# The first attention's start: order of loads, a key mask built on the chip, and the place of batch 1's work

## The reference, cut to what matters

```python
x = x + _L0_xattn_ref(_layernorm(x), ctx_4096, ctx_4096, Wq, Wk, Wv, Wo)
# inside: 32 query heads of 16, 8 key/value heads of 16, each shared by 4 query heads
q = (query @ Wq).reshape(b, sq, 32, 16).transpose(0, 2, 1, 3)
k = (key @ Wk).reshape(b, sk, 8, 16).transpose(0, 2, 1, 3)
v = (value @ Wv).reshape(b, sk, 8, 16).transpose(0, 2, 1, 3)
k, v = jnp.repeat(k, 4, axis=1), jnp.repeat(v, 4, axis=1)
probs = jax.nn.softmax(jnp.einsum('bhqd,bhkd->bhqk', q, k) * 16 ** -0.5, axis=-1)
out = jnp.einsum('bhqk,bhkd->bhqd', probs, v)      # then merged and multiplied by Wo
```

## Time and profile before

| | |
|---|---|
| median of 3 runs | 1506.38 us (1503.81, 1506.38, 1508.53) |
| the profiled execution's own time | 1510.69 us |
| its span in the trace | 1508.9 us, 31382 instructions |
| busy, whole span | PE 92%, VectorE 72%, ScalarE 51%, GpSimd 48% |
| first attention | starts the program; its last work ends near 170.8 us |

### The profile page before, as it was taken

The page is one execution under the profiler, slowest core; times in us unless marked ns, Lnnn a source line. Parts: engine busy times, 40 slices in busy tenths (PEclk is TensorE's granted clock), DMA queues, the critical chain, the costliest instruction groups (busy, mean ns, idle before and its releaser), DMA issues.

```text
span 1508.9 us, 31382 instructions
## 1 busy us (share of the span) xinstructions
PE 1392.4 (92%) x11352; PEld 831.1 (55%) x11352; DVE 1080.5 (72%) x2125; ACT 762.5 (51%) x2476; POOL 721.8 (48%) x748
## 2 busy tenths in 40 slices
PE   5898699997999999897999999999999788889998
PEld 5676344445777777544655555555555334434444
DVE  7998655645666666767989888898877888965212
ACT  4777363222434333347666666666665457655111
POOL 4887452001434443855666666666665405734000
PEclk9999699999999999999999999999999899999999
DMA  7999672124999988766766665756534401646000
GB/s 192 188 173 169 130 179 43 32 39 116 179 186 188 172 139 138 133 145 156 155 150 112 114 112 110 144 112 111 110 71 80 133 3 29 131 84 112 22 8 28
DMA packets 524569, 174.62 MB, mean 116 GB/s; under 512 B 482576, under 2 KB 507600, under 8 KB 524416
## 3 DMA queue, kind: packets, MB, share of 16 engines
q1 hardware_dynamic: 524416, 172.62, 59.3%
HBM read 53.27 MB, written 2.10 MB: 37 GB/s over the span
## 4 chain that ended last, share of the span: by engine, by line
PE 70%; DVE 10%; POOL 7%; issue 4%; DMA 4%; ACT 3%; SPq 1%; DVEq 0%; PEld 0%; ACTq 0%; POOLq 0%; PEldq 0%
PE bank L70 22%; PE bank L72 22%; PE bank L71 22%; DMA a_p_t<-a_p_hl 2%; PE bank L2787 1%; DVE stats L111 1%; POOL a_p_hl L691 1%; DVE a_negmax L595 1%; DVE a_p_hl L602 1%; POOL x_o_prod L3108 1%; POOL x_o_prod L3109 1%; POOL down_flat L3351 1%; POOL x_state L3101 1%; DMA a_q_t<-a_q_hl 0%; PE bank L1025 0%
## 5 line engine op out<-in xcount | busy, mean ns | idle before, releaser
L1913 POOL TENSOR_TENSOR a_q_ss<-a_q_ss,half 128x4 f32<-128x4 f32 x64 | 90.2, 1409 | 167.4 <-DVE a_q_ss L1822 83.9
L1735 ACT ACTIVATE a_probs<-a_masked,a_negmax 128x128 f32<-128x128 f32 x256 | 99.7, 391 | 101.4 <-DVE a_negmax L1793 101.4
L70 PE MATMUL bank<-a_wq_hi,xn_pair 128*128 128x512 f16 (+1 forms) x384 | 140.2, 365 | 7.9 <-DVE a_kn L1827 3.1
L1256 POOL TENSOR_TENSOR a_p_hl<-a_probs,a_p_hl 128x512 f16<-128x512 f32 x64 | 74.4, 1164 | 143.2 <-DVE a_p_hl L1180 143.2
L71 PE MATMUL bank<-a_wq_lo,xn_pair 128*128 128x512 f16 (+1 forms) x384 | 139.9, 364 | 0.0
L72 PE MATMUL bank<-a_wq_hi,xn_pair 128*128 128x512 f16 (+1 forms) x384 | 139.9, 364 | 0.0
L70 PE MATMUL bank<-a_wo_hi,a_o_hi 128*128 128x512 f16 x256 | 97.8, 382 | 4.4 <-DVE x_state L1809 3.5
L72 PE MATMUL bank<-a_wo_hi,a_o_lo 128*128 128x512 f16 x256 | 97.7, 382 | 0.0
L71 PE MATMUL bank<-a_wo_lo,a_o_hi 128*128 128x512 f16 x256 | 97.6, 381 | 0.0
L1928 POOL TENSOR_TENSOR a_normal<-a_probs,a_recip 128x512 f32<-128x512 f32 x64 | 90.3, 1410 | 5.0
L691 POOL TENSOR_TENSOR a_p_hl<-a_probs,a_p_hl 128x512 f16<-128x512 f32 x64 | 77.3, 1219 | 25.4 <-DVE a_p_hl L602 19.3
(11 more groups left out here) (467 smaller groups left out, 5029.9 us busy)
## 6 DMA issues: line engine op xcount, KB each, us to landing
a_no<-in_L_xattn_Wo SPq DMA_DIRECT2D x9, 1024.0 KB, 6.0
a_nq<-in_L_xattn_Wq SPq DMA_DIRECT2D x8, 1024.0 KB, 5.8
a_n_wq<-in_L_xattn_Wq SPq DMA_DIRECT2D x4, 768.0 KB, 5.1
a_n_wo<-in_L_xattn_Wo SPq DMA_DIRECT2D x4, 768.0 KB, 5.6
a_nk<-in_L_xattn_Wk SPq DMA_DIRECT2D x9, 256.0 KB, 3.0
a_nv<-in_L_xattn_Wv SPq DMA_DIRECT2D x9, 256.0 KB, 4.0
f_v_hat<-in_L_ffn_w SPq DMA_DIRECT2D x2, 1152.0 KB, 6.2
x_state<-in_x SPq DMA_DIRECT2D x8, 256.0 KB, 4.8
```

The costliest lines, as they stand in the source:

```text
L70: pe.matmul(out, lh, rh, start=start, stop=False)
L1256: pool.tensor_tensor(p_hl[s % PN][:, 1, t, :], probs[unit(s, t) % PROBS][:, :, :].rearrange("p h n -> p (h n)"), p_hl[s % PN][:, 0, t, :], ...
L1735: m = act.activation(probs[s % 2][:, h, :], src, ACT.Exp, bias=negmax[s % 2][:, h:h + 1], accum_out=total[s % 2][:, h:h + 1])
L1913: pool.tensor_tensor(r[:, :], r[:, :], K.half[:, 0:n], ALU.pow).then_inc(root_done.sem, 1)
```

## The change

The constants of batches 1 and 2 get delays (LATE), used through late_at in place of at for five kinds of step: batch 1's normalising moves from t = -8 to -3, its rows from -6 to -2, its context from -5 to -1, its keys on the PE from -1 to 2, their high half on ScalarE from -2 to 3, their masking from -1 to 3; batch 2's normalising from 0 to 3 and its rows from 2 to 4. The statistics of batches 2 and 3 move from t = -2 to 2. Batch 1's x and context are loaded at t = -13, behind the first transpose and the value weight; the transpose of batch 1 now stands behind the output weight's load. The last two quarters of the query weight are split at t = -11, ahead of batch 0's keys. The mask is no longer loaded: GpSimd makes a 128 x 8 tile with a memset and two affine selects, each waiting for the one before, ahead of its other constants, and the product reads each of its values 128 times. Steps of batches 3 to 7 keep their places.

```diff
-    WEIGHTS = (-13, -12, -11, -10, -9, -7, 2, 3, 4, 5)
+    WEIGHTS = (-13, -12, -11, -11, -11, -7, 2, 3, 4, 5)
+    LATE = {"norm": {1: 5, 2: 3}, "rows": {1: 4, 2: 2}, "ctx": {1: 4}, "keys": {1: 3}, "keys split": {1: 5}, "mask": {1: 4}}
-    R1, R2, R3 = -9, -2, 11
-    LX1, LV, LX2, LO, LX4 = -16, -14, -6, -6, 4
+    R1, R2, R3 = -9, 2, 11
+    LX1, LV, LX2, LO, LX4 = -13, -14, -6, -6, 4
-        keep = sb("keep", [P, KV, P], F16)
+        keep = sb("keep", [P, KV], F16)
+        late_at = lambda t, offset, kind: [b for b in range(B) if t == offset + UNITS * b + LATE[kind].get(b, 0)]
...
-            sp.dma_start(keep[:, :, :], keep_in).then_inc(keep_here, 16)
...
-                for b in at(t, KPROJ):
+                for b in late_at(t, KPROJ, "keys"):
                     keys(b)
...
                 if b == 0:
-                    dve.wait_ge(keep_here, 16)
+                    dve.wait_ge(keep_done, 3)
...
                     r = dve.tensor_tensor(k_m[b % 2][:, a, :, :], k_hl[b % 2][:, a, :].unsqueeze(1).to_broadcast([P, KV, P]),
-                                          keep[:, :, :], ALU.mult)
+                                          keep[:, :].unsqueeze(2).to_broadcast([P, KV, P]), ALU.mult)
...
             roots(0)
+            pool.memset(keep[:, :], 1.0).then_inc(keep_done, 1)
+            pool.wait_ge(keep_done, 1)
+            pool.affine_select(out=keep[:, :], in_=keep[:, :], compare_op=ALU.is_ge, fill=0.0,
+                               base=0, pattern=[[-D, KV]], channel_multiplier=1).then_inc(keep_done, 1)
+            pool.wait_ge(keep_done, 2)
+            pool.affine_select(out=keep[:, :], in_=keep[:, :], compare_op=ALU.is_ge, fill=0.0,
+                               base=D - 1, pattern=[[D, KV]], channel_multiplier=-1).then_inc(keep_done, 1)
```

More of the change, by code:

```diff
@@ L179, in load_first, with first_attention @@
         sp.dma_start(self.n2[:, :, :], self.w2.rearrange("(f p) d -> p f d", p=P)[:, 0:2, :]).then_inc(self.first_in, 16)
-def first_attention(K, front, x_in, ctx_t, keep_in, wq, wk, wv, wo):
+def first_attention(K, front, x_in, ctx_t, wq, wk, wv, wo):
     nc = K.nc
@@ L249, in first_attention @@
         max_done, plo_done, mixed = per_unit("max"), per_unit("plo"), per_unit("mixed")
-        const_done, ones_done, keep_here = sem("const"), sem("ones"), sem("keep_in")
+        const_done, ones_done, keep_done = sem("const"), sem("ones"), sem("keep")
         two = lambda n: [sem(f"{n}{i}") for i in range(2)]
@@ L339, in _ @@
                     load_context(1)
-                for b in at(t, XLO):
+                for b in late_at(t, XLO, "rows"):
                     turn_queries_in(b)
@@ L348, in _ @@
                         load_x(b)
-                for b in at(t, CTX):
+                for b in late_at(t, CTX, "ctx"):
                     if b + 2 < B:
@@ L498, in _ @@
                     high_of_queries(b)
-                for b in at(t, KSPLIT):
+                for b in late_at(t, KSPLIT, "keys split"):
                     high_of_keys(b)
@@ L634, in _ @@
                     low_of_values(b)
-                for b in at(t, KMASK):
+                for b in late_at(t, KMASK, "mask"):
                     masked_keys(b)
@@ L642, in _ @@
                         take_stats(b0, b1)
-                for b in at(t, CTX):
+                for b in late_at(t, CTX, "ctx"):
                     high_of_context(b)
-                for b in at(t, XHI):
+                for b in late_at(t, XHI, "rows"):
                     high_of_rows(b)
@@ L650, in _ @@
                     add_to_x(b)
-                for b in at(t, NORM):
+                for b in late_at(t, NORM, "norm"):
                     normalise(b)
@@ L3699, in stage_0_to_1 @@
         front = Front(K, c, *(a[f"L0_ffn_{w}"] for w in ("c1_w", "c2_w", "w1", "w2t")))
-        first_attention(K, front, a["x"], a["ctx_t"], a["keep"], *(a[f"L0_xattn_{w}"] for w in ("Wq", "Wk", "Wv", "Wo")))
+        first_attention(K, front, a["x"], a["ctx_t"], *(a[f"L0_xattn_{w}"] for w in ("Wq", "Wk", "Wv", "Wo")))
         K.end_stage()
@@ L3750, in tables @@
     vspec[P - 1] = np.stack([np.cos(rest).sum(0), -np.sin(rest).sum(0)])
-    keep = np.broadcast_to((i[:, None] // 16 == np.arange(8))[:, :, None], (P, 8, P)).astype(np.float16)
     f = lambda v: np.ascontiguousarray(v, np.float32)
     return {"hadamard": np.stack([h, -h], axis=1), "spec": f(spec), "inv": f(inv), "pspec": f(pspec),
-            "oinv": f(oinv), "keep": keep, "vspec": f(vspec)}
+            "oinv": f(oinv), "vspec": f(vspec)}
 def laid_out(inputs):
```

## The result

The changed kernel takes 1515.5 us (median of 6 runs, 1513.3 to 1518.8) against 1507.9 for the kernel before on the same chip (6 runs): a ratio of 1.005, 95% interval 1.0038 to 1.0061, so 5.7 to 9.2 us slower. Forecast were +6.2 us, 1512.6 us by the sum, and a slower kernel.

What follows compares the result with a forecast made beforehand. VectorE's pace was taken to bound the first attention from some 27 us on. -0.4 (fill) + 7.6 (14 products) - 1.0 (waits) = +6.2 us on 1506.4, so 1512.6; own range +3.7 to +9.1, all cases 1506.0 to 1517.0.

Steps and rivals of the forecast that it cites:

- The price of the mask: VectorE's masking products: each goes from 679 to 1220 ns with the mask standing still; 14 of them cost 7.6 us.
- Rival A: The masking product keeps its 679 ns, so only the fill counts: 1506.0 us; chance 0.12.
- The waits that would give 1.0 us back: VectorE's 2.5 us of waits for batches' keys and values shrink by 1.0 us, bounds 0 and 2.5.
- rival C: GpSimd's next subtraction goes between the two products of a pair, 1.15 us each for three pairs: +10.7 us, 1517.1; chance 0.11.
- Rival B: Product takes 1220 ns, but VectorE's shrinking waits for GpSimd and others absorb much of it: +1.0 us, 1507.4; chance 0.15.
- The fill: Start of the first attention, rearranged: worth 0.4 us (-0.4), bounds 2.5 us won to 1.5 us lost.
- Rival D: The first maxima's 3.2 us gain lasts to the end, product at 679 ns: -4.2 us, 1502.2; chance 0.03.
- The first transpose: Ahead of the first query projection: 1.1 to 1.4 us won, 0.45 to 0.7 lost; projection starts about 12.2, 0.5 us sooner.

Runs made afterwards that it cites:

- e2: The kernel before with only the small mask, built by GpSimd and read standing still, start order unchanged; ratio 1.0067 to before.
- e1: The changed kernel with the wide mask loaded from the host again, all else of the change kept; ratio 1.0014 to before.
- e8: The changed kernel with its small mask stored twice side by side (128 x 8 x 2) and read in pairs; ratio 0.9994 to 1.0017 to before.
- e7: The changed kernel with GpSimd copying its small mask once into a wide tile that the products read; ratio 1.0005 to before.
- e9: The changed kernel's mask in pairs, with only batch 1's keys late and the output weight loaded ahead of batch 1's transpose; ratio 1.0004 to before.
- e5: The kernel before with batch 1's keys late, and batches 2 and 3's x and the output weight loaded ahead of batch 1's transpose; ratio 0.9986 to before.
- e6: The kernel before with one of VectorE's four casts of probabilities per batch given to ScalarE; ratio 0.9993 to before.
- e4: The kernel before with only batch 1's keys, their split and their masking moved behind the first scores; ratio 0.9995 to 1.0020 to before.

## Why the prediction was right, and where it was off

**The price of the mask: right.** Forecast 541 ns per product from the nearest rows; the shortest differ by 1216 - 679 = 537. Fourteen of them were 7.6 us by the sum; e2, which has no other edit, shows 6.8 to 13.4 us by its interval, e1, which has all but this, 0.2 to 4.1. The rule of the Trainium skill on the innermost step (Vector Engine (DVE) Microarchitecture Reference, section 5.1), cited as the one that speaks against the change, agrees: 1216 ns with a step of zero, 676 with a pair that steps by one (e8). Rival A is refuted.

**The waits that would give 1.0 us back: mis-sized.** From batch 2's masking to batch 7's the change takes 5.2 us more (85.64 against 80.44), and ten products of 537 ns more are 5.4. So all else together gave back 0.2 us, not 1.0. The waits named went from 2.5 to 2.2 us only. The casts of the probabilities shortened by 0.8 us in sum. Against that stands batch 6's pair of products, which now met GpSimd and took 1.34 us more. That is a piece of rival C, for one pair instead of three. Rival B is refuted: it put the change at +1.0 us, and the interval begins at 5.7. Its idea, that VectorE's waits for GpSimd would shrink with the load, has that 0.8 us for it, where it asked for 3.7.

**The fill: batch 1's late transpose right, the PE's clock left out.** The first scores came at 17.59 (18.6 forecast) and the first maxima at 18.97 (20.0 to 20.6). The projection began at 11.84, not 12.2, and its pace doubled at 15.0, 3.2 us into it, where before that came at 17.3, 4.6 us into it (the PE's timeline after; three matmuls take 0.32 us, then 0.17):

```profile
11.84 0.27 PE L70 MATMUL bank<-a_xn_t,a_wq_hi 128*128 128x128 f16 x1 [0.22 <-DVE a_wq_lo L525]
...
14.67 0.31 PE L70 MATMUL bank<-a_xn_t,a_wq_hi 128*128 128x128 f16 x1
...
14.99 0.23 PE L70 MATMUL bank<-a_xn_t,a_wq_hi 128*128 128x128 f16 x1
...
15.17 0.22 PE L70 MATMUL bank<-a_xn_t,a_wq_hi 128*128 128x128 f16 x1
```

What brought that forward is open. Just ahead of the projection the PE rested 0.22 us instead of 1.51, but in e2 it rested 0.42 there and the pace still doubled only 5.05 us into the projection.

The fourth scores started at 25.87, where 25.8 was forecast, and that agreement is luck. The transpose was late for the reason given, but the PE had it at 23.36 and not at 24.3; then the queries' quarter and the keys took 2.5 us at 1.2 GHz, where 1.5 had been put. At the same clock the scores themselves ended near 27.3, and the fourth maxima came at 27.39 instead of 26.5. e7, with the same order and a rest of 3.73 us, kept the full clock (first its PE, then its VectorE, then its stretch, in the columns of the earlier trace rows):

```profile
23.07 0.22 PE L70 MATMUL bank<-a_xn_t,a_wq_hi 128*128 128x128 f16 x1 [3.73 <-issue]
```
```profile
25.27 0.69 DVE L596 TENSOR_REDUCE a_negmax<-bank 128x4 f32<-128x512 f32 x1 [2.07 <-PE bank L72]
```
```profile
23.00:28.40 5.40, 5.33 (x79) 5.16 (x80) 3.33 (x8) 2.62 (x8) 2.76 (x4) 1.00 1.10 135
```

Its fourth scores began at 24.41 and its fourth maxima at 25.27. Rival D ends here too: it needed batch 1's transpose before 22.5, and in no trace of this order did the PE have it before 23.07.

With batch 1's longer pair (1.1) taken off, batch 2's masking is 1.4 us late in the change. In the three kernels that have its order and short products it is 0.1 us early where the clock stayed up (e7), and 0.4 and 0.8 us late where it was at 0.50 for 3.4 us (e8, e1); in the change it was at 0.50 for 5.2 us. So the term of -0.4 is some 0.3 us from what was measured at the full clock, and what it left out is the clock: 0.5 to 1.5 us, if all of the distance from e7 is put down to it. Both small terms were off the same way, the fill by 1.8 us and what was to be given back by 0.8. In the trace the change stood 8.8 us behind at the end of the last masking and 9.6 at the next stage; the runs show 7.6, and the sum had 6.2. The sum came out on its large term. The lower end of the forecast's own range was added up wrongly: from bounds of -2.5 for the fill and -2.5 for the waits it is +2.6, not +3.7.

**The first transpose: right.** GpSimd's mask, on its timeline after:

```profile
5.59 0.10 POOL L703 MEMSET a_keep<- 128x8 f16 x1
5.77 0.19 POOL L705 TENSOR_SCALAR_AFFINE_SELECT a_keep<-a_keep 128x8 f16<-128x8 f16 x1
6.03 0.26 POOL L708 TENSOR_SCALAR_AFFINE_SELECT a_keep<-a_keep 128x8 f16<-128x8 f16 x1
...
7.16 1.31 POOL L682 TENSOR_TENSOR a_xn_hl<-a_xn,a_xn_hl 128x512 f16<-128x512 f32 x1
```

It took 0.64 us (0.8 forecast), and the low half of the rows began 0.40 late (0.45), 0.18 of which is x landing later (statistics at 3.64 instead of 3.46). The transpose was issued at 8.50 and landed 3.2 us later; at 11.84 the PE was waiting not for it but for a quarter of the weight. So the landing of 4.5 us did shrink once the three loads stood behind: it took 4.5 to 4.9 us in the six traces that have all three ahead, 3.8, 3.6 and 3.4 in those with one or two (e9, e1, e2), and 3.2 in the three with none. The masking of batch 0 ended at 14.9 and held up nothing, as forecast; in the order of the kernel before it did (e2).

**Open:** what bounds the stretch when VectorE has time to spare, as in e5 and e6. Open too is what decides whether the PE's clock falls: the change, e1, e7 and e8 rested 3.63, 3.71, 3.73 and 3.73 us, and e7 alone stayed at 1.00.

## What to carry to other kernels

Before a tile is replaced by a broadcast of a smaller one, look at which dimension stands still: a 16-bit product of two operands kept its double rate here with an outer dimension of step zero (the keys, all along) and with a repeated pair, and lost it with an innermost step of zero; a mask stored twice costs 32 bytes. In an in-order pipeline that runs at one engine's pace, a faster start is worth only what that engine's next wait lets through, so name the next late thing (here batch 1's transpose in the change, the output weight in e4) before counting the gain. And test a bound in both directions: this stretch charged in full for time added to VectorE and showed no gain for time taken from it.

## What the runs showed that was not expected

A stretch of the PE after 3.6 us of rest ran at half the granted clock for over 5 us (0.50 from 23.3 to 28.4), just where the next work of VectorE stood waiting. It is nothing that the change brought: the kernel before had the same after its rest of 1.95 us, under its first scores (columns of the earlier trace rows):

```profile
21.20:24.00 2.80, 2.80 (x16) 2.01 (x14) 2.21 (x5) 0.36 (x2) 0.60 (x1) 0.50 0.85 201
```

The length of the rest alone doesn't decide: e7 rested 3.73 us and kept the full clock. And pairs of products that meet GpSimd take 1.34 us more whether a product lasts 0.68 or 1.22 us.
